# A four-layer hybrid block on one core: the engine loop written out, a new order of pieces, and a last chunk with a second V layout

## Chip, core and metric

The kernel runs on one NeuronCore of a Trainium2 chip. The metric is the device time of one execution in microseconds (us). TensorE (PE) multiplies, VectorE (DVE), ScalarE (ACT) and GpSimd (POOL) do the rest, and SyncE (SP) issues most of the transfers.

## What is computed

The input x is 8 batches x 512 tokens x 128 features, float32. Four layers follow, each added to x after a layer norm of x:

```
x = x + ssm(layernorm(x))      # 8 heads of 64 values, state 128; B and C turned by cumulative angles
x = x + ffn(layernorm(x))      # x @ ternary(W).T * alpha + bias, 128 -> 128
x = x + attn(layernorm(x))     # 16 heads of 8, over the 8 batches of each token
x = x + ffn(layernorm(x))      # the same ternary weights
```

The ssm layer is a scan over the 512 tokens of a batch (h = alpha h + beta Bx_prev + gamma Bx, y = h.C), an RMS norm and an output projection. The attention softmax has only 8 columns, the batches of one token.

## The kernel before

Every engine has a program of its own, and semaphores tie them. The tokens are cut into 4 chunks of 128 (NC = 4); a chunk has 8 tiles, one per batch, each 128 tokens x 128 features. A tile is worked in two **units** of four heads, so a chunk has 16 units (UNITS) and unit k belongs to tile k//2. The ssm of a unit on TensorE: project_b and project_c (three passes of 128x512 each), ScalarE turns the result by cosine and sine (L922, L937), GpSimd adds the two parts (L630, L631), TensorE transposes (L1679), scores (L1816); VectorE scans the decays into a mask (scan, L1282) from a band that GpSimd made (band_of, L651) and multiplies the scores by it (weigh_scores, writes mmat, L1290); TensorE makes outputs (L1829, L1835) and states (L1848); VectorE adds up y (L1301, L1304) and the state (L1321). After two units ScalarE squares y (L958), VectorE sums the squares (L1330), TensorE projects out (L1858, L1859), and VectorE copies the result to oraw (o_out, L1334).

Layers 2 to 4 of a chunk are small **pieces** (norms, transposes, FFN products, score products "prod", their sums "red", softmax) that run among the units of the next chunk. The table PLACE (L66) gives each a place in units; at 16 and over it falls in the next chunk. step() of each engine lays down the calls of one unit and, between them, at_span() lets the pieces of a stretch in. run_chunks (L130) calls step():

```python
    with eng.Fori(1, NC - 1) as c:
        for k in range(UNITS):
            step(c, k, pieces)
```

Chunk 0 and chunk 3 are written out; chunks 1 and 2 are two passes of one hardware loop, on all five engines (SP's at L516). In the loop some waits and addresses come from registers.

Chunk 3 has no chunk after it. Its first FFN and its attention start as **head pieces** (names with h, by pairs p of tiles): rms root, x1, norm hnorm0, transpose hT0, FFN hF, hadd, hnorm1, hT1, then hKV, hQ and the products hprod and sums hred of the scores that need no tile of pair 3. What is left is the **ending**, written by hand: the lists TV, TA, TP, TG number the steps of VectorE, ScalarE, TensorE and GpSimd. scores_of and sum_copied finish the scores, weights() makes the softmax in two halves, values_of(s) (DVE L1598, POOL L801) multiplies weights by V into a 128x1024 tile for each batch tile s, and add_rows (L2049) lets TensorE add its 8 parts with 8 matmuls against the identity. GpSimd makes the values of tiles 2 to 5, VectorE those of 0, 1, 6, 7; the last two VectorE first folds from 1024 to 256 (L1603), so that they take 2 matmuls each. Then for each pair: out_of (L2054), attended (DVE L1608, L1614, L1619), a root on GpSimd (L809), norm_of (L1625), turn_pair (L2073), ffn_of (L2054), add_to_x and the store.

Warm-up matmuls (keep_warm, L1679 with only ident) keep TensorE occupied while it waits.

## Time and profile before

| | us |
|---|---|
| three runs | 607.63, 604.37, 606.64; median 606.64 |
| profiled execution | 608.52 |
| its span | 606.8 |
| PE busy | 526.3 (87%) |
| ACT busy | 482.5 (80%) |
| DVE busy | 470.1 (77%) |
| POOL busy | 433.8 (71%) |
| mean granted TensorE clock | 0.966 |

The span is what the profiler saw from the first to the last event on the core; 1.7 us of the execution lie around it. In the rows below a timeline line has its start in us, its length in us, engine, line, operation, tiles, forms, and in brackets how long the engine was idle before it and what ended that; a window line has its ends and length, then busy us (instructions) of PE, PEld (weight loads), DVE, ACT, POOL, then the mean clock, the DMA share and GB/s. Busy shares are means over stretches that differ: set-up to 45 us, chunk 0 to about 140, chunks 1 and 2 of about 140 each, chunk 3 with the head pieces to about 560, then the ending.

### The profile page before, as it was taken

What the parts mean: (1) busy time and instruction counts of PE and PEld (TensorE: products, weight loads), DVE (VectorE), ACT (ScalarE), POOL (GpSimd) and SP (SyncE); (2) the same over time, 40 slices, a digit from 0 to 9 for tenths busy, and PEclk for the clock granted to TensorE, in tenths of its full rate; (3) what the DMA queues carried; (4) which work ended last, traced back from release to release, by engine and by line L of the source; (5) the groups of instructions that cost most, each with busy time, mean ns of one, the idle gap of its engine ahead of it and who ended that gap; (6) DMA issues with size and microseconds to landing.
All of it is one profiled execution on the core that took longest, in us unless ns stands there. A gap on an engine that the chain in (4) does not pass through costs nothing. (4 is left out here: it accounts for less than half of the span.)

```text
span 606.8 us, 13457 instructions
## 1 busy us (share of the span) xinstructions
PE 526.3 (87%) x3932; PEld 437.9 (72%) x3932; DVE 470.1 (77%) x1093; ACT 482.5 (80%) x1478; POOL 433.8 (71%) x568
## 2 busy tenths in 40 slices
PE   5978999999999898896999888899998786879287
PEld 4866888888887777785887777788777575766175
DVE  6666576687659999983767999997559979953995
ACT  3799999999998879695998887789999789843101
POOL 7348777878777887783678796977768876944742
PEclk9989999999999999997999999999999989987769
DMA  8841222132111112231111111232211112000001
GB/s 198 219 112 50 75 74 81 59 99 76 59 44 52 59 59 59 62 102 35 56 59 59 59 53 31 93 94 93 88 31 54 63 41 66 27 18 2 1 0 36
DMA packets 52309, 39.44 MB, mean 65 GB/s; under 512 B 7301, under 2 KB 48010, under 8 KB 52234
## 3 DMA queue, kind: packets, MB, share of 16 engines
q1 hardware_dynamic: 45898, 35.39, 19.7%
q10 hardware_dynamic: 6336, 3.15, 1.8%
q8 instruction: 36, 0.59, 0.4%
q14 instruction: 39, 0.32, 0.2%
HBM read 33.44 MB, written 4.46 MB: 62 GB/s over the span
## 5 line engine op out<-in xcount | busy, mean ns | idle before, releaser
L937 ACT ACTIVATE turned<-ps,sct 128x128 f32<-128x128 f32 x376 | 110.7, 446 | 0.0
L922 ACT ACTIVATE turned<-ps,sct 128x128 f32<-128x128 f32 x368 | 103.3, 434 | 6.4 <-DMA sct<-packed 3.9
L1282 DVE TENSOR_TENSOR_SCAN lmat<-arow,band 128x512 f32<-128x512 f32 x64 | 86.5, 1356 | 5.6 <-POOL band L651 3.6
L630 POOL TENSOR_TENSOR cn<-turned 128x256 f32<-128x256 f32 x64 | 54.4, 850 | 39.4 <-ACT turned L937 39.4
L1290 DVE TENSOR_TENSOR mmat<-ps,lmat 128x512 f32<-128x512 f32 x64 | 43.9, 685 | 46.4 <-PE ps L1816 46.4
L630 POOL TENSOR_TENSOR bn<-turned 128x256 f32<-128x256 f32 x64 | 52.9, 826 | 36.7 <-PE ps L1848 25.1
L1816 PE MATMUL ps<-cT,bT 128*128 128x128 f32 x512 | 69.4, 278 | 8.2 <-DVE state L1321 5.8
L1816 PEld LDWEIGHTS ps<-cT,bT 128*128 128x128 f32 x512 | 63.2, 191 | 16.4 <-issue 14.9
L828 ACT ACTIVATE area<-ps 128x256 f32<-128x256 f32 (+1 forms) x68 | 34.6, 565 | 42.8 <-PE ps L2049 14.0
L1721 PE MATMUL ps<-w_sel_hi,xt_hi 128*128 128x512 f32 x128 | 59.1, 462 | 1.4 <-ACT turned L937 1.4
L1848 PE MATMUL ps<-wu,bn 128*128 128x128 f32 x384 | 54.6, 286 | 4.0 <-DVE mmat L1290 3.9
L828 ACT ACTIVATE cT<-ps 128x512 f32<-128x512 f32 x64 | 43.7, 683 | 13.8 <-PE ps L1679 13.3
L1848 PEld LDWEIGHTS ps<-wu,bn 128*128 128x128 f32 x384 | 47.3, 194 | 9.5 <-issue 9.3
L631 POOL TENSOR_TENSOR bn<-turned 128x256 f32<-128x256 f32 x64 | 53.1, 830 | 0.0
L1679 PE MATMUL ps<-ident,cn 128*128 128x128 f32 x256 | 40.4, 281 | 14.4 <-ACT bT L828 14.1
L828 ACT ACTIVATE bT<-ps 128x512 f32<-128x512 f32 x64 | 43.5, 679 | 11.5 <-PE ps L1679 11.5
L651 POOL TENSOR_TENSOR band<-bandm,sct 128x512 f32<-128x512 f32 x48 | 50.3, 1049 | 1.3 <-DMA sct<-packed 1.3
L1723 PE MATMUL ps<-w_sel_hi,xt_lo 128*128 128x512 f32 x128 | 50.8, 397 | 0.0
L1722 PE MATMUL ps<-w_sel_lo,xt_hi 128*128 128x512 f32 x128 | 50.7, 396 | 0.0
L631 POOL TENSOR_TENSOR cn<-turned 128x256 f32<-128x256 f32 x64 | 49.9, 780 | 0.0
L1829 PE MATMUL ps<-mmat,u_nat 128*64 128x128 f32 x512 | 42.6, 288 | 6.9 <-DVE mmat L1290 6.6
L1679 PEld LDWEIGHTS ps<-ident,cn 128*128 128x128 f32 x256 | 28.7, 142 | 21.9 <-issue 21.3
(271 smaller groups left out, 1430.1 us busy)
## 6 DMA issues: line engine op xcount, KB each, us to landing
arow<-alpha_rows SPq DMA_DIRECT2D x32, 512.0 KB, 3.7
drow<-decay_rows SPq DMA_DIRECT2D x64, 128.0 KB, 3.1
area<-in_L_attn_a_x_dram SPq DMA_DIRECT2D x4, 512.0 KB, 6.1
xT_rows<-turned SPq DMA_DIRECT2D x4, 512.0 KB, 4.9
xt<-xT_rows SPq DMA_DIRECT2D x32, 64.0 KB, 2.5
area<-in_L_attn_a_x_dram ACTq DMA_DIRECT2D x6, 256.0 KB, 3.0
out_dram<-area ACTq DMA_DIRECT2D x6, 256.0 KB, 2.4
area<-L_attn_a_sel_proj_w_dram SPq DMA_DIRECT2D x2, 512.0 KB, 6.4
```

What stands on the lines that cost most here:

```text
L630: pool.tensor_tensor(out[:, 0], zc[:, 0], zs[:, 1], ALU.subtract)
L631: return pool.tensor_tensor(out[:, 1], zc[:, 1], zs[:, 0], ALU.add)
L828: return act.activation(dst, src, ACT.Copy)
L922: last = act.activation(dst[h][:, N * q:N * q + N], bank(BK_B)[:, N * q:N * q + N], ACT.Copy, scale=scalars(c, k)[:, at + HH * h + q:at + ...
L937: last = act.activation(dst[h][:, N * q:N * q + N], bank(BK_C)[:, N * q:N * q + N], ACT.Copy, scale=scalars(c, k)[:, at + HH * h + q:at + ...
L1282: dve.tensor_tensor_scan(lmat[h], arow[i2][:, HH * P * h:HH * P * (h + 1)], band[h], 0.0, ALU.mult, ALU.add).then_inc(l_dve, 1)
L1679: last = pe.transpose(bank(k)[:, into + P * q:into + P * q + P], s, ident[:])
L1721: pe.matmul(out, xt_hi[i2], hi, start=True, stop=False)
L1722: pe.matmul(out, xt_hi[i2], lo, start=False, stop=False)
L1723: pe.matmul(out, xt_lo[i2], hi, start=False, stop=True).then_inc(signal, 1)
L1816: last = pe.matmul(bank(BK_G)[:, P * q:P * q + P], bT[h][:, P * q:P * q + P], cT[h][:, P * q:P * q + P], start=True, stop=True)
L1848: last = pe.matmul(bank(BK_G)[:, at:at + P], bn[h][:, N * q:N * q + N], wu[h][:, 2 * PD * (q // 2):2 * PD * (q // 2) + 2 * PD], start=True ...
```

## The change

1. The loop over chunks 1 and 2 is written out on all five engines. No register is computed and no branch taken there; every wait is for a constant. The load of ScalarE's function table, which stood in the first step of the loop body and ran in each pass, now stands once, ahead of the first softmax exponential, in chunk 1.
2. The table PLACE and the order of calls in step() are new. VectorE's o_out stands before weigh_scores in even units, its scan of an even unit at the end of the odd one before, GpSimd's band_of one place earlier, TensorE's outputs always before states. Many head pieces of chunk 3 are earlier.
3. In the last chunk ScalarE writes V out a second time as vals_er, with the 8 batches innermost. It does so in f_hvals, after a wait until the stores of chunk 2 have landed, since vals_er lies over their rows. The values of tiles 4 to 7 are made in this layout, and VectorE sums each over the batches with one reduce (128x1024 to 128x128); TensorE then turns each with one transpose. The folds on VectorE go. GpSimd folds tiles 2 and 3 once, so that they take 4 matmuls each instead of 8.
4. Warm-up transposes: 8 before the last project_out, 24 before the ending's first rows, 4 before its second.
5. out_of and ffn_of use other PSUM banks by pair, and the ending's steps are in a new order on VectorE and TensorE.

```diff
-WARM_STATS, WARM_NORM, WARM_SCALARS, WARM_ANGLE, WARM_LAST = 4, 1, 4, 2, 1
+WARM_STATS, WARM_NORM, WARM_SCALARS, WARM_ANGLE, WARM_LAST, WARM_VALUES = 4, 1, 4, 2, 1, 2
...
-PLACE = {"hrms:0": 10.75, "hx1:0": 10.786, "rr:0": 11.296, "hroot0:0": 11.407, "hnorm0:0": 11.441,
+PLACE = {"hx1:0": 6.844, "hrms:0": 6.917, "hroot0:0": 7.444, "hnorm0:0": 9.276, "rr:0": 11.148, "hrms:1": 11.259,
...
-    with eng.Fori(1, NC - 1) as c:
+    for c in range(1, NC - 1):
...
+ON_GPSIMD_LAST = [2, 3, 4, 5]
-               ("v", 6), ("v", 7), ("a", 6), ("a", 7), ("h", 6), ("h", 7),
-               ("ao", 0), ("st", 0), ("mv", 0), ("ao", 1), ("st", 1), ("mv", 1),
-               ("xn", 0), ("xn", 1), ("ao", 2), ("st", 2), ("mv", 2), ("ao", 3), ("st", 3), ("mv", 3),
-               ("af", 0), ("af", 1), ("xn", 2), ("xn", 3), ("af", 2), ("af", 3)])
...
+        vals_er = area[:, 3072:4096].rearrange("p (e r) -> p e r", r=NB)
...
-        o_bank = [bank(BK_C), bank(BK_Y), bank(BK_C), bank(BK_Y)]
-        ffn_bank = [bank(BK_F0), bank(BK_M), bank(BK_F1), bank(BK_T)]
+        o_bank = [bank(BK_C), bank(BK_Y), bank(BK_F0), bank(BK_M)]
+        ffn_bank = [bank(BK_C), bank(BK_Y), bank(BK_F1), bank(BK_T)]
...
                 if first_chunk(c):
                     pool.wait_ge(pv, PV["packed"])
-                elif k < 0:
+                else:
                     scalars_ready(pool, c, k)
...
             def values_of(s):
                 pool.wait_ge(tv, TV["wp", s // 4])
...
+                else:
+                    tick(pool.tensor_tensor(wide[s].rearrange("p (h d r) -> p h d r", r=NB, d=AD),
+                                            w_last[:, s - 2, :].rearrange("p (h r) -> p h r", r=NB).unsqueeze(2).broadcast_to([P, AH, AD, NB]),
+                                            vals_er.rearrange("p (h d) r -> p h d r", d=AD), ALU.mult), ("v", s))
...
+            def fold(s):
+                pool.wait_ge(tg, TG["v", s])
+                tick(pool.tensor_tensor(wide[s][:, 0:512], wide[s][:, 0:512], wide[s][:, 512:1024], ALU.add), ("a", s))
...
             values_of(2)
+            fold(2)
             values_of(3)
+            fold(3)
             values_of(4)
             values_of(5)
...
             def f_hvals(c, p):
                 act.wait_ge(hp[p], HEAD_P["KV"])
-                evac(vals_last[:, pair(p), :], kv_bank[p].rearrange("p (s e) -> p s e", s=2)[:, :, D:2 * D]).then_inc(ha[p], 1)
+                rows = kv_bank[p].rearrange("p (s e) -> p s e", s=2)[:, :, D:2 * D]
+                evac(vals_last[:, pair(p), :], rows)
+                for g in range(2):
+                    act.wait_ge(rows_free[g], 16 * NC)
+                evac(vals_er[:, :, pair(p)].rearrange("p e s -> p s e"), rows).then_inc(ha[p], 1)
...
@@ VectorE, step(), even units, both forms cut to the calls @@
-                    scan(c, k)
-                    y_of(c, k - 2)
-                    weigh_scores(c, k - 1)
-                    o_out(c, (k - 4) // 2)
+                    y_of(c, k - 2)
+                    o_out(c, (k - 4) // 2)
+                    weigh_scores(c, k - 1)
@@ TensorE, step(), odd units, likewise @@
-                    states(c, k - 1)
-                    outputs(c, k - 1)
+                    outputs(c, k - 1)
+                    states(c, k - 1)
...
-            def fold(s, n, before, name):
-                dve.wait_ge(tv, TV[before, s])
-                end_tick(dve.tensor_tensor(wide[s][:, 0:n], wide[s][:, 0:n], wide[s][:, n:2 * n], ALU.add), (name, s))
...
+            def sum_values(s):
+                if s in (4, 5):
+                    dve.wait_ge(tg, TG["v", s])
+                else:
+                    dve.wait_ge(tv, TV["v", s])
+                end_tick(dve.tensor_reduce(xn[:, s], wide[s].rearrange("p (e r) -> p e r", r=NB), AX.X, ALU.add), ("r", s))
 
...
-            fold(6, 512, "v", "a")
-            fold(7, 512, "v", "a")
-            fold(6, 256, "a", "h")
-            fold(7, 256, "a", "h")
+            sum_values(4)
+            sum_values(5)
+            sum_values(6)
             attended(0)
+            sum_values(7)
             attended(1)
             norm_of(0)
+            attended(2)
             norm_of(1)
-            attended(2)
             attended(3)
             add_to_x(0, ffn_bank[0], "F", "af")
+            norm_of(2)
             add_to_x(1, ffn_bank[1], "F", "af")
-            norm_of(2)
             norm_of(3)
             add_to_x(2, ffn_bank[2], "F", "af")
...
+                if in_ending(c) and b == NB - 1:
+                    for signal, count in ((y_dve, UNITS * NC), (ysq_act, NT)):
+                        pe.wait_ge(signal, count)
+                        keep_warm(WARM_LAST, BK_T)
...
-                if s in (2, 3, 4, 5):
-                    pe.wait_ge(tg, TG["v", s])
+                if s in ON_GPSIMD_LAST:
+                    pe.wait_ge(tg, TG["v" if n == NB else "a", s])
                 else:
-                    pe.wait_ge(tv, TV["v" if n == NB else "h", s])
+                    pe.wait_ge(tv, TV["v", s])
...
+            def turn_row(p, s):
+                pe.wait_ge(tv, TV["r", s])
+                at = P * (s % 2)
+                return pe.transpose(acc_bank[p][:, at:at + P], xn[:, s], ident[:])
+
...
+            for name in ("sum", "rec", "w"):
+                pe.wait_ge(tv, TV[name, 0])
+                keep_warm(WARM_VALUES, BK_C)
             add_rows(0, 0, NB)
+            pe.wait_ge(tv, TV["sub", 1])
+            keep_warm(WARM_LAST, BK_C)
             end_tick(add_rows(0, 1, NB), ("acc", 0))
-            add_rows(1, 2, NB)
-            end_tick(add_rows(1, 3, NB), ("acc", 1))
+            bias_of(o_bank[0], BIAS_O)
+            bias_of(o_bank[1], BIAS_O)
+            add_rows(1, 2, NB // 2)
+            end_tick(add_rows(1, 3, NB // 2), ("acc", 1))
             out_of(0)
             out_of(1)
-            pe.wait_ge(tv, TV["v", 1])
-            bias_of(ffn_bank[0], BIAS_F)
-            bias_of(ffn_bank[1], BIAS_F)
-            add_rows(2, 4, NB)
-            end_tick(add_rows(2, 5, NB), ("acc", 2))
-            pe.wait_ge(tv, TV["w", 1])
-            bias_of(ffn_bank[2], BIAS_F)
-            add_rows(3, 6, 2)
-            end_tick(add_rows(3, 7, 2), ("acc", 3))
-            bias_of(ffn_bank[3], BIAS_F)
-            out_of(2)
-            out_of(3)
-            turn_pair(0)
-            turn_pair(1)
-            ffn_of(0)
-            ffn_of(1)
-            turn_pair(2)
-            turn_pair(3)
-            ffn_of(2)
-            ffn_of(3)
+            for p in (2, 3):
+                bias_of(o_bank[p], BIAS_O)
+            for p in (2, 3):
+                turn_row(p, 2 * p)
+                end_tick(turn_row(p, 2 * p + 1), ("acc", p))
+                out_of(p)
+            for p in (0, 1):
+                pe.wait_ge(tv, TV["ao", p])
+                bias_of(ffn_bank[p], BIAS_F)
+            for p in (2, 3):
+                bias_of(ffn_bank[p], BIAS_F)
+            for p in range(4):
+                turn_pair(p)
+                ffn_of(p)
```

How the instructions stand. First TensorE where chunk 1 begins, before:

```order
L1679 MATMUL ps<-ident,bn 128x128 x4
L136 UNCONDITIONAL_BRANCH
L136 ISA
L1679 MATMUL ps<-ident,area 128x128 x4
L1824 REGISTER_ALU
L1825 REGISTER_ALU
L243 REGISTER_ALU
L1829 MATMUL ps<-mmat,u_nat 64x128 x4
L243 REGISTER_ALU
L1835 MATMUL ps<-cT,state 64x128 x4
L1848 MATMUL ps<-wu,bn 128x128 x4
L1804 REGISTER_ALU
```

and after:

```order
L1744 MATMUL ps<-w_sel_lo,xt_hi 128x512
L1745 MATMUL ps<-w_sel_hi,xt_lo 128x512
L1701 MATMUL ps<-ident,area 128x128 x4
L1701 MATMUL ps<-ident,bn 128x128 x4
L1851 MATMUL ps<-mmat,u_nat 64x128 x4
L1857 MATMUL ps<-cT,state 64x128 x4
L1870 MATMUL ps<-wu,bn 128x128 x4
L1701 MATMUL ps<-ident,cn 128x128 x4
```

The branch, the ISA row (of the loop) and the register rows are gone; outputs (L1829, L1835, now L1851, L1857) and states (L1848, now L1870) keep their order in this unit, and the transposes of area (L1679, now L1701) have moved before those of bn.

Second, VectorE after the last unit of chunk 3; L1452 (now L1466) is hadd, L1446 (now L1460) is hnorm0 and hnorm1, L1461 (now L1475) is a product of scores. Before, from hadd of pair 2 on:

```order
L1452 TENSOR_TENSOR small<-ps,small 128x256
L1431 BN_STATS stats_h<-small 128x6 x2
L1434 MEMSET carrier 128x1
L1436 BN_AGGR mv_h<-stats_h 128x2 x2
L1446 TENSOR_SCALAR area<-small,mv_h,rs_h 128x128 x2
L1452 TENSOR_TENSOR small<-ps,small 128x256
L1431 BN_STATS stats_h<-small 128x6 x2
L1434 MEMSET carrier 128x1
L1436 BN_AGGR mv_h<-stats_h 128x2 x2
L1446 TENSOR_SCALAR area<-small,mv_h,rs_h 128x128 x2
L1461 TENSOR_TENSOR area<-ps,area 128x1024
L1461 TENSOR_TENSOR area<-ps,area 128x512
```

and after, from the end of x1 of pair 3 on:

```order
L1448 MEMSET carrier 128x1
L1450 BN_AGGR mv_h<-stats_h 128x2 x2
L1460 TENSOR_SCALAR area<-small,mv_h,rs_h 128x128 x2
L1466 TENSOR_TENSOR small<-ps,small 128x256
L1445 BN_STATS stats_h<-small 128x6 x2
L1448 MEMSET carrier 128x1
L1450 BN_AGGR mv_h<-stats_h 128x2 x2
L1475 TENSOR_TENSOR area<-ps,area 128x512
L1475 TENSOR_TENSOR area<-ps,area 128x1024
L1480 TENSOR_REDUCE area<-area 128x2x4x16
L1480 TENSOR_REDUCE area<-area 128x2x2x16
L1460 TENSOR_SCALAR area<-small,mv_h,rs_h 128x128 x2
```

hadd of pair 2 now stands before the copy of the last oraw and so no longer between x1 of pair 3 and hnorm0 of pair 3; the products hprod4 and hprod3 and two sums have moved before hnorm1 of pair 3.

Third, VectorE in the ending, from the values of tiles 6 and 7 on. Before:

```order
L1598 TENSOR_TENSOR arow<-ps,area 128x1024 x2
L1603 TENSOR_TENSOR arow<-arow 128x512 x2
L1603 TENSOR_TENSOR arow<-arow 128x256 x2
L1608 TENSOR_TENSOR small<-ps,small 128x256
L1614 BN_STATS stats_f<-small 128x6 x2
L1617 MEMSET carrier 128x1
L1619 BN_AGGR mv_f<-stats_f 128x2 x2
L1608 TENSOR_TENSOR small<-ps,small 128x256
L1614 BN_STATS stats_f<-small 128x6 x2
L1617 MEMSET carrier 128x1
L1619 BN_AGGR mv_f<-stats_f 128x2 x2
L1625 TENSOR_SCALAR area<-small,mv_f,rs_f 128x128 x4
```

and after:

```order
L1616 TENSOR_TENSOR arow<-ps,area 128x1024 x2
L1625 TENSOR_REDUCE area<-area 128x128 x2
L1625 TENSOR_REDUCE area<-arow 128x128
L1630 TENSOR_TENSOR small<-ps,small 128x256
L1636 BN_STATS stats_f<-small 128x6 x2
L1639 MEMSET carrier 128x1
L1641 BN_AGGR mv_f<-stats_f 128x2 x2
L1625 TENSOR_REDUCE area<-arow 128x128
L1630 TENSOR_TENSOR small<-ps,small 128x256
L1636 BN_STATS stats_f<-small 128x6 x2
L1639 MEMSET carrier 128x1
L1641 BN_AGGR mv_f<-stats_f 128x2 x2
```

Four folds (L1603) have given way to four reduces (L1625), and the last of these stands after the first attended.

## Rows read from the trace of the kernel before

**Rows 1.** Windows: each engine's busy us (instructions), clock, DMA; chunks 1, 2, ending
```profile
149.20:281.20 132.00, 117.16 (x919) 97.68 (x920) 110.89 (x242) 112.16 (x348) 99.07 (x125) 0.99 0.19 60
289.50:421.50 132.00, 122.20 (x965) 102.38 (x964) 114.23 (x259) 115.13 (x358) 103.34 (x130) 1.00 0.22 66
560.00:607.00 47.00, 28.53 (x177) 23.90 (x176) 35.77 (x69) 6.75 (x18) 23.07 (x17) 0.82 0.04 12
```

**Rows 2.** Timeline of VectorE: mmat of units around chunk boundaries (start, us, idle before)
```profile
140.34 0.69 DVE L1290 TENSOR_TENSOR mmat<-ps,lmat 128x512 f32<-128x512 f32 x1 [0.17 <-PE ps L1816]
...
149.22 0.69 DVE L1290 TENSOR_TENSOR mmat<-ps,lmat 128x512 f32<-128x512 f32 x1 [0.28 <-PE ps L1816]
...
276.30 0.68 DVE L1290 TENSOR_TENSOR mmat<-ps,lmat 128x512 f32<-128x512 f32 x1
...
289.49 0.69 DVE L1290 TENSOR_TENSOR mmat<-ps,lmat 128x512 f32<-128x512 f32 x1 [0.26 <-PE ps L1816]
...
414.32 0.68 DVE L1290 TENSOR_TENSOR mmat<-ps,lmat 128x512 f32<-128x512 f32 x1
...
421.49 0.69 DVE L1290 TENSOR_TENSOR mmat<-ps,lmat 128x512 f32<-128x512 f32 x1 [0.27 <-PE ps L1816]
```

**Rows 3.** Timeline of TensorE, ScalarE and GpSimd where chunk 1 becomes chunk 2
```profile
276.58 0.33 PE L1679 MATMUL ps<-ident,area 128*128 128x128 f32 x1 [2.09 <-issue]
...
279.83 0.80 PE L1679 MATMUL ps<-ident,area 128*128 128x128 f32 x3 [2.92 <-issue]
...
277.24 1.28 ACT L828 ACT_TABLE_LOAD   x1 [1.50 <-issue]
...
284.71 0.73 POOL L630 TENSOR_TENSOR bn<-turned 128x256 f32<-128x256 f32 x1 [10.19 <-PE ps L1848]
```

**Rows 4.** Timeline of ScalarE, first step of chunk 1
```profile
143.48 1.28 ACT L828 ACT_TABLE_LOAD   x1
```

**Rows 5.** The page's costliest groups: outputs and band (count, busy, mean ns, idle before)
```profile
L1829 PE MATMUL ps<-mmat,u_nat 128*64 128x128 f32 x512 | 42.6, 288 | 6.9 <-DVE mmat L1290 6.6
...
L651 POOL TENSOR_TENSOR band<-bandm,sct 128x512 f32<-128x512 f32 x48 | 50.3, 1049 | 1.3 <-DMA sct<-packed 1.3
```

**Rows 6.** Timeline of TensorE and VectorE, last tile of chunk 3
```profile
536.21 1.06 PE L1858 MATMUL ps<-w_out,yT 128*128 128x128 f32 x8
...
543.31 2.08 PE L1858 MATMUL ps<-w_out,yT 128*128 128x128 f32 x8 [2.69 <-DVE ysum L1330]
...
547.23 0.61 DVE L1424 SCALAR_TENSOR_TENSOR small<-oraw,rr_h,small 128x128 f32<-128x128 f32 x2 [1.08 <-POOL rr_h L722]
...
552.32 0.42 DVE L1452 TENSOR_TENSOR small<-ps,small 128x256 f32<-128x256 f32 x1 [2.56 <-PE ps L1938]
...
553.46 0.57 DVE L1446 TENSOR_SCALAR area<-small,mv_h,rs_h 128x128 f32<-128x128 f32 x2
```

**Rows 7.** Timeline of VectorE and ScalarE, from pair 3 to the first late scores
```profile
558.33 0.60 DVE L1446 TENSOR_SCALAR area<-small,mv_h,rs_h 128x128 f32<-128x128 f32 x2 [1.08 <-POOL rs_h L730]
...
561.86 1.82 DVE L1461 TENSOR_TENSOR area<-ps,area 128x1024 f32<-128x1024 f32 x2 [2.93 <-PE ps L1956]
...
564.88 0.38 ACT L828 ACTIVATE q_last<-ps 128x256 f32<-128x256 f32 x1 [0.41 <-PE ps L1956]
...
568.98 1.22 DVE L1461 TENSOR_TENSOR area<-ps,area 128x1024 f32<-128x1024 f32 x1 [0.19 <-issue]
```

**Rows 8.** Timeline of VectorE and GpSimd, last values to the end
```profile
570.23 1.22 DVE L1466 TENSOR_REDUCE area<-area 128x128 f32<-128x1024 f32 x1
...
584.43 3.90 POOL L801 TENSOR_TENSOR area<-w_last,area 128x1024 f32<-128x1024 f32 x2 [4.34 <-DVE w_last L1578]
...
586.98 3.16 DVE L1603 TENSOR_TENSOR arow<-arow 128x512 f32<-128x512 f32 x4
...
598.20 0.42 DVE L1608 TENSOR_TENSOR small<-ps,small 128x256 f32<-128x256 f32 x1 [3.08 <-PE ps L2054]
...
603.55 0.94 DVE L1608 TENSOR_TENSOR small<-ps,small 128x256 f32<-128x256 f32 x2 [1.20 <-PE ps L2054]
```

187 lines of the change are left out of this document (94 added, 93 removed), and 65 rows, old and new, of tables (PLACE, TV).

## Prediction

> **What bounds the kernel now.** I read four views in this order: busy time by windows, to see what is full in each chunk; VectorE's timeline around each chunk boundary; the timelines of all engines across the last tile of chunk 3; and those of the ending. In the windows [rows 1] no engine is full in chunks 1 and 2: of 132.0 us, TensorE is busy 117 and 122, ScalarE 112 and 115, VectorE 111 and 114. Two chunks with 5 us difference in TensorE work take the same 132.0 us, so TensorE's sum alone doesn't set the pace; it is the round of waits from unit to unit, and a queue change pays or costs where the reader would look for it last. In the ending [rows 1] TensorE is busy 28.5 of 47 us at a clock of 0.82, VectorE 35.8: there VectorE leads, with some waits.
>
> The unit rows [rows 2] show what the windows hide. The multiply of scores (mmat) starts in the last unit of a chunk and in the first of the next at 276.30 and 289.49 (13.19 us apart) between chunks 1 and 2, at 414.32 and 421.49 (7.17) between 2 and 3, where the same pieces run but no branch is taken, and at 140.34 and 149.22 (8.88) where the loop is entered. First unit to first unit is 140.27 and 132.00 us; the difference is 8.27. So each pass back costs 8.3 us. The engines say what it is [rows 3]: TensorE sits idle 2.09 and 2.92 us "issue", that is for nothing the profile shows, inside a group of four transposes; ScalarE has 1.50 us of the same and a table load of 1.28; GpSimd waits 10.19 us for TensorE. The page "Runtime: NRT & Kernel Launch" of the Trainium skill (Instruction fetch mechanics) says that a taken branch out of the fetched window has to fetch its target before it can go on, and that straight code is prefetched at a mostly hidden cost; the stall at the branch agrees, and boundary 2 to 3 shows none in straight code.
>
> **The change, part by part.** All against the profiled execution, 608.52 us.
>
> 1. Loop written out: the back edge goes, **-8.3**. At the entry, 8.88 - 7.17 = 1.7 us are there to gain; of it the table load of 1.28 [rows 4] is on ScalarE, which has no idle time there. It moves to where VectorE is ahead of it in chunk 1, and one of its two runs goes. I take **-1.3** (bounds: 0 and -1.7). Register instructions go in 32 units; the page gives them no time: nothing taken.
>
> 2. New order and table. Unit order stays nearly the same. On VectorE o_out goes ahead of mmat in even units, on TensorE outputs ahead of states in all. o_out waits for project_out, which TensorE issues ahead of the scores that mmat waits for, so this costs the copy alone, hidden where mmat waits anyway. GpSimd's band (1.05 us [rows 5]) is made earlier, and costs only if it delays an add. Moved pieces keep their durations. Each of three chunks may move by some us either way: VectorE idles 132.0 - 114.2 = 17.8 us in chunk 2 [rows 1]. That is an upper bound for a gain in a chunk, and nothing in the rows gives a direction; nearest is that chunks 1 and 2, with different piece loads, took the same time. I take **0**, with 3 us to either side per chunk for three chunks.
>
> 3. Last tile. The last project_out takes 2.08 us, the one before 1.06 [rows 6]: it came after a wait of 2.69 and ran at half clock. Warmed, it gives **-1.0**. Then x1 of pair 3 (547.23) is ready for its norm about 1.3 + 1.1 us later, 549.6, but the norm starts at 553.46, since VectorE first waits 2.56 us for hadd of pair 2 [rows 6]. That wait goes. What is late next is TensorE: behind project_out stand hT1 of pair 1, hQ of pair 0, hKV and hQ of pair 1 and 12 warm-ups. Before, 7.8 us lay between the end of the norm (554.0) and the product that ended VectorE's wait at 561.86 [rows 7]: about 2.0 for transpose, copy and product of pair 3, and five hKV or hQ groups, so 1.16 each. So three groups (3.5), a transpose with its copy (0.8) and 12 warm-ups (1.6, at 1.06 for eight [rows 6]) are 5.9 us from 544.7, and pair 3's transpose can start at about 550.6 against 554.0. hadd of pair 3 comes at 552.5; only hT1, hKV and hQ of pair 2 (0.8 and two groups, 3.1) stand before hprod4 and hprod3, so these start at about 555.6 against 561.86 [rows 7]. Here the change gives something back: hnorm1 of pair 3 now stands behind two products (1.82 [rows 7]) and two sums (as long again), and comes at 559.2 against 558.33, 0.9 us later. But before, TensorE was then busy with pairs 1 and 2 until 561.9; now it is free, and pair 3's K and Q come 3 us earlier. The norm (0.6) and three sums (3.5 us) follow on VectorE, and the first late scores come at 563.3 against 568.98 [rows 7]: **-5.7 in all, the -1.0 within it**. q_last (564.88) comes at about 562.9, so GpSimd's two scores stay ahead of their readers. Bounds: -3 if TensorE runs this at half clock, -8 if the warm-ups cost nothing. ScalarE's four second copies of V (0.4 to 0.7 us each) and the wait for chunk 2's stores lie in ScalarE's idle time; uncovered they cost 2 us.
>
> 4. Ending. Until v7 VectorE does the same work in the same order, with one wait less between parts: 0. Behind it (586.98 [rows 8]) it did four folds (3.16), then waited 3.08 for pair 2's product and 1.20 for the last [rows 8]. Now: four reduces of 128x1024 at 1.22 [rows 8], less overlap 4.8; four attended at 1.14 (552.32 to 553.46 is such a triple [rows 6]), 4.6; four norms at 0.60 [rows 7], 2.4; four final adds at 0.47 [rows 8], 1.8. That is 13.6 with no wait, so 600.6, and the last norm is still followed by transpose, copy and product, 1.2 as before: 601.8 against 603.55 + 0.94 = 604.5, **-2.7**. It is covered if GpSimd has v4 and v5 by 590: before 584.43 + 3.90 = 588.3 [rows 8], and its two new folds (128x512, like the band's 1.05 [rows 5]) end before the weights of half 1. Bounds: 0, and -4.3 if both waits go with nothing in return. The sum uses the row. A rule of the Trainium skill speaks against the reduce: "VectorE: DVE Perf Modes" (Rules for kernel authors) calls tensor_reduce the slowest VectorE operation and advises to restructure. The row differs: 1.22 us for 1024 elements [rows 8], the same as the multiply at 568.98 [rows 7]. Were the reduce twice as slow, the sum would lose 4.9 and the ending would end 2 us later than before.
>
> Sum: -8.3 - 1.3 - 5.7 - 2.7 = -18.0, so 590.5 for an execution like the profiled one. That one lies 1.9 above the median of the three runs (606.64), so I forecast **588.6**.
>
> **Rivals.**
> - *The new order also gains* (chance 0.16): less waiting for scores, 2 to 3 us per chunk: 580 to 583. For: 17.8 us idle on VectorE. Against: TensorE waited only 6.6 us for mmat in all 64 units [rows 5].
> - *Last tile and ending give back* (0.20): TensorE stays at half clock through pair 3, reduces or the new V layout are slow, or ScalarE's wait for the stores delays the last square. Then only the loop's 9.6 and a rest remain: 592 to 598. For: clock 0.82 in the ending. Against: the reduce's row.
> - *The straight code stalls by itself* (0.05): the fetch of more code costs as much as the branch: 597 to 600. Against: no such stall at 414 to 421.
> - *The order costs* (0.06): 2 to 4 us per chunk, 594 to 600.
> - *Slower* (0.04): TensorE's outputs now stand ahead of states everywhere, and so wait for mmat, with the next unit's transposes behind them. Now 9 waits, 6.6 us in all [rows 5], 0.73 each. Should each of 48 units wait 0.73 us, that is +28: 616. It decides from a loss of 18.0 + 3, 0.44 us per unit, or 29 waits more. Against: in half of the units outputs stand there already.
>
> The forecast itself, 584 to 592, has 0.49.
>
> **Chances and range.** About 0.5% (3 us) is what a measurement of this kernel tells from no change. Faster: 0.49 + 0.16 + 0.20 + 0.05 and nearly all of "costs", 0.94; same 0.02; slower 0.04. The range, 580 to 598, leaves out a better order than 3 us per chunk (0.03) and the last of the rivals (some 0.12).
>
> **What would show it.** First units of chunks 132 us apart with no "issue" wait and no table load at the start of chunk 1 (step 1); the same distances off by 1 to 3 us (step 2); project_out of the last tile at 1.1 us, hnorm0 of pair 3 within 3 us of x1, the first late scores 18 us behind the last oraw, which is now at 547.2 - 1.1 - 0.3 = 545.8 [rows 6], 23.1 us ahead of them (step 3); no wait over 1.5 us on VectorE between v7 and the end, and 14.8 us from v7's end to VectorE's last add against 17.5 (step 4). The prediction is wrong if the first units stay 140 us apart, or if units of chunk 3 take longer than before.

## The result, and the profile after

The changed kernel takes **599.88 us** (median of 7 runs, 598.03 to 601.9); before takes 606.64 (7 runs, 602.45 to 608.08). The ratio is 0.9906, with a 95% interval from 0.988 to 0.9932: 6.8 us faster, where 18.0 were forecast. The measured time lies outside the range of 580 to 598.

The profiled execution of the changed kernel has 598.75 us and a span of 597.0. Before, span and execution were 606.8 and 608.52. So the two profiled executions differ by 9.8 us, 3 more than the medians, since one lies 1.9 us above its median and the other 1.1 below. VectorE's first mmat starts between 50.05 and 52.45 us in the 18 profiled executions of this document, with no relation to what the kernels change, so a difference of 1 to 2 us between two single executions says nothing of the edit. Stage by stage, from the start of one VectorE instruction to the next (unit numbers count from 0 to 63; "end" is the end of VectorE's last add):

| from, to | before | after | forecast of the difference | measured |
|---|---|---|---|---|
| mmat of unit 0, unit 15 | 89.37 | 89.36 | 0 | 0 |
| 15, 16 (loop entry) | 8.88 | 7.62 | -1.3 | -1.3 |
| 16, 32 (chunk 1 and the back edge) | 140.27 | 131.95 | -8.3 | -8.3 |
| 32, 48 (chunk 2) | 132.00 | 132.03 | 0 | 0 |
| 48, 63 (chunk 3) | 116.93 | 121.39 | 0 | **+4.5** |
| 63, first reciprocal | 36.44 | 30.38 | -5.7 | -6.1 |
| first reciprocal, second | 8.32 | 8.92 | 0 | **+0.6** |
| second reciprocal, end | 21.31 | 22.69 | -2.7 | **+1.4** |

The first mmat also starts 0.5 us earlier. The forecast's four terms came out at -8.3, -1.3, -6.1 and, for the ending, +2.0; the part that was put at nothing cost 4.5. The sixth row goes past the point at which step 3 of the forecast ends: from mmat of unit 63 to the first late scores 30.56 us became 24.08, -6.5, and 0.4 us were lost again before the reciprocal.

The windows of chunk 2 and of the end, columns as in [rows 1]:

```profile
279.40:411.40 132.00, 122.32 (x965) 102.42 (x964) 113.86 (x259) 114.75 (x357) 101.22 (x129) 1.00 0.22 66
...
575.80:597.00 21.20, 12.63 (x51) 8.37 (x49) 12.53 (x41) 2.69 (x7) 5.63 (x9) 0.61 0.09 26
```

Chunk 2 is as full as before [rows 1]. The last 21 us run at a clock of 0.61.

VectorE's timeline, the same units as in [rows 2] and then units 61 to 63:

```profile
139.78 0.68 DVE L1304 TENSOR_TENSOR mmat<-ps,lmat 128x512 f32<-128x512 f32 x1
...
147.40 0.69 DVE L1304 TENSOR_TENSOR mmat<-ps,lmat 128x512 f32<-128x512 f32 x1 [0.27 <-PE ps L1838]
...
272.25 0.68 DVE L1304 TENSOR_TENSOR mmat<-ps,lmat 128x512 f32<-128x512 f32 x1
...
279.35 0.69 DVE L1304 TENSOR_TENSOR mmat<-ps,lmat 128x512 f32<-128x512 f32 x1 [0.26 <-PE ps L1838]
...
404.29 0.68 DVE L1304 TENSOR_TENSOR mmat<-ps,lmat 128x512 f32<-128x512 f32 x1
...
411.38 0.69 DVE L1304 TENSOR_TENSOR mmat<-ps,lmat 128x512 f32<-128x512 f32 x1 [0.27 <-PE ps L1838]
...
517.57 0.68 DVE L1304 TENSOR_TENSOR mmat<-ps,lmat 128x512 f32<-128x512 f32 x1
...
525.80 0.69 DVE L1304 TENSOR_TENSOR mmat<-ps,lmat 128x512 f32<-128x512 f32 x1 [2.30 <-PE ps L1838]
...
532.77 0.69 DVE L1304 TENSOR_TENSOR mmat<-ps,lmat 128x512 f32<-128x512 f32 x1 [0.33 <-PE ps L1838]
```

The three boundaries are now 7.62, 7.10 and 7.09 us long. Unit 62 comes 8.23 us after unit 61, with VectorE idle 2.30 for scores. Before, the mmat of unit 61 started at 526.24 and that of unit 62 came 5.2 us after it:

```profile
531.43 0.69 DVE L1290 TENSOR_TENSOR mmat<-ps,lmat 128x512 f32<-128x512 f32 x1 [1.02 <-PE ps L1816]
```

So 3.0 of the 4.5 us of chunk 3 lie in this one interval. In the changed kernel, the timelines of ScalarE and TensorE show what TensorE waited for there:

```profile
517.63 0.88 ACT L1049 ACTIVATE small<-small,sh_h,rs_h 128x128 f32<-128x128 f32 x2 [2.69 <-POOL sh_h L734]
...
521.32 0.66 ACT L841 ACTIVATE bT<-ps 128x512 f32<-128x512 f32 x1
...
522.12 0.63 PE L1701 MATMUL ps<-ident,cn 128*128 128x128 f32 x4 [1.42 <-ACT bT L841]
```

ScalarE stood 2.69 us before a head norm, for GpSimd's shift. Behind it in its queue were the turn of B of unit 63 and the copy bT of unit 62, and TensorE's transposes of C waited for that copy.

GpSimd was late for a reason of its own. Two of its instructions on 128x2 took 1.02 and 1.15 us, where the same two took 0.20 and 0.19 for the pair before (at 512.73 and 512.89). They ran while VectorE did two scans, and each ended where a scan ended:

```profile
514.37 2.31 DVE L1296 TENSOR_TENSOR_SCAN lmat<-arow,band 128x512 f32<-128x512 f32 x2
...
514.54 1.02 POOL L727 TENSOR_TENSOR rs_h<-mv_h,eps_ln 128x2 f32<-128x2 f32 x1 [0.51 <-DVE mv_h L1450]
515.52 1.15 POOL L729 TENSOR_SCALAR sh_h<-mv_h 128x2 f32<-128x2 f32 x1
```

That is 1.8 of ScalarE's 2.69 us. The same pair of long instructions (1.02 and 1.14 to 1.15 us) stands there in all nine profiles that keep this root and these scans in their new places. No experiment moved a scan; e9_norm0b below moved the root away from them and met another wait. So what the kernel would take without this meeting alone is not shown.

The other 1.5 us are spread out: 0.8 in units 48 to 53 and 0.7 in units 53 to 61. In the latter VectorE is nearly full, busy 61.6 of 64.3 us after and 60.2 of 63.6 before, so head pieces that are moved there have little idle time to run in.

The last tile, to lay beside [rows 6] and [rows 7]:

```profile
537.69 1.16 PE L1884 MATMUL ps<-w_out,yT 128*128 128x128 f32 x8
...
540.48 0.61 DVE L1438 SCALAR_TENSOR_TENSOR small<-oraw,rr_h,small 128x128 f32<-128x128 f32 x2 [1.08 <-POOL rr_h L723]
...
542.98 0.61 DVE L1460 TENSOR_SCALAR area<-small,mv_h,rs_h 128x128 f32<-128x128 f32 x2 [1.08 <-POOL rs_h L731]
...
548.77 1.82 DVE L1475 TENSOR_TENSOR area<-ps,area 128x512 f32<-128x512 f32 x2 [1.60 <-PE ps L1982]
...
552.36 0.60 DVE L1460 TENSOR_SCALAR area<-small,mv_h,rs_h 128x128 f32<-128x128 f32 x2
...
553.01 0.68 PE L1956 MATMUL ps<-ident,area 128*128 128x128 f32 x2 [3.94 <-DVE area L1460]
...
556.85 1.23 DVE L1475 TENSOR_TENSOR area<-ps,area 128x1024 f32<-128x1024 f32 x1 [0.51 <-ACT area L841]
```

project_out is at full clock (1.16 us). The norm of pair 3 (542.98) starts 2.50 us after its x1 (540.48), where it was 6.2 [rows 6]. The products start at 548.77, the second norm stands behind them at 552.36, TensorE waits 3.94 us for it, and the first late scores start at 556.85.

The ending, beside [rows 8]:

```profile
573.16 4.67 POOL L807 TENSOR_TENSOR area<-w_last,area 128x1024 f32<-128x1024 f32 x2 [1.72 <-DVE w_last L1592]
...
575.73 1.21 DVE L1625 TENSOR_REDUCE area<-area 128x128 f32<-128x1024 f32 x1
...
577.87 1.22 DVE L1625 TENSOR_REDUCE area<-area 128x128 f32<-128x1024 f32 x1 [0.93 <-POOL area L807]
...
585.57 0.69 PE L2100 MATMUL ps<-ident,area 128*128 128x128 f32 x2
...
586.73 1.22 PE L2084 MATMUL ps<-w_of,area 128*128 128x128 f32 x4 [0.47 <-ACT area L841]
...
587.98 0.42 DVE L1630 TENSOR_TENSOR small<-ps,small 128x256 f32<-128x256 f32 x1 [1.14 <-PE ps L2084]
...
590.10 0.42 DVE L1630 TENSOR_TENSOR small<-ps,small 128x256 f32<-128x256 f32 x1 [1.18 <-PE ps L2084]
...
594.34 0.42 DVE L1630 TENSOR_TENSOR small<-ps,small 128x256 f32<-128x256 f32 x1 [1.70 <-PE ps L2084]
```

GpSimd's two values in the new layout take 4.67 us against 3.90 [rows 8], and VectorE waits 0.93 for the second. One value takes 2.35 to 2.37 us in the new layout and 1.97 in the old one, in before, the changed kernel, e3, e10 and e15 alike, so this is the layout's price. At the end TensorE's two transposes take 0.69 and four products 1.22, both at half clock, with 0.47 idle between them for ScalarE's copy. The final adds start 2.12 us apart (587.98, 590.10, 592.22, 594.34), each after a wait of over a microsecond.

### The profile page after: what moved, and what is told of

Its sections match the earlier page's. It is cut to its first block, busy times and chain, and to the rows that moved or that the text cites. A ratio compares the mean times of both kernels' runs of the same rounds, so it can differ in the third digit from the quotient of the medians.

```text
span 597.0 us, 12795 instructions
## 1 busy us (share of the span) xinstructions
PE 524.3 (88%) x3916; PEld 432.6 (72%) x3916; DVE 473.0 (79%) x1093; ACT 481.9 (81%) x1481; POOL 436.1 (73%) x570
## 4 chain that ended last, share of the span: by engine, by line
PE 42%; DVE 34%; ACT 9%; issue 9%; POOL 5%; DMA 1%; DVEq 1%; SPq 0%; ACTq 0%; POOLq 0%
PE ps L1701 7%; PE ps L1870 5%; PE ps L1838 5%; DVE lmat L1296 5%; PE ps L1851 3%; DVE area L1403 3%; PE ps L1743 3%; PE ps L1745 3%; PE ps L1744 3%; DVE state L1335 3%; PE ps L1884 2%; DVE mmat L1304 2%; DVE area L1386 2%; ACT turned L950 2%; ACT turned L935 2%
## 5 line engine op out<-in xcount | busy, mean ns | idle before, releaser
L1296 DVE TENSOR_TENSOR_SCAN lmat<-arow,band 128x512 f32<-128x512 f32 x64 | 82.4, 1291 | 3.6 <-POOL band L652 3.6
L631 POOL TENSOR_TENSOR bn<-turned 128x256 f32<-128x256 f32 x64 | 49.7, 776 | 38.2 <-PE ps L1870 31.7
L1304 DVE TENSOR_TENSOR mmat<-ps,lmat 128x512 f32<-128x512 f32 x64 | 43.9, 686 | 41.4 <-PE ps L1838 41.3
L631 POOL TENSOR_TENSOR cn<-turned 128x256 f32<-128x256 f32 x64 | 50.3, 786 | 29.9 <-ACT turned L950 29.6
L841 ACT ACTIVATE area<-ps 128x256 f32<-128x256 f32 (+1 forms) x72 | 37.9, 576 | 39.0 <-PE ps L2100 8.1
L632 POOL TENSOR_TENSOR bn<-turned 128x256 f32<-128x256 f32 x64 | 58.0, 906 | 0.0
L1851 PE MATMUL ps<-mmat,u_nat 128*64 128x128 f32 x512 | 42.1, 285 | 15.5 <-DVE mmat L1304 15.5
L1870 PE MATMUL ps<-wu,bn 128*128 128x128 f32 x384 | 55.6, 288 | 0.0
L1870 PEld LDWEIGHTS ps<-wu,bn 128*128 128x128 f32 x384 | 46.5, 191 | 8.2 <-issue 8.2
L632 POOL TENSOR_TENSOR cn<-turned 128x256 f32<-128x256 f32 x64 | 51.9, 811 | 0.0
L1701 PE MATMUL ps<-ident,cn 128*128 128x128 f32 x256 | 39.4, 276 | 9.9 <-ACT bT L841 8.7
L1851 PEld LDWEIGHTS ps<-mmat,u_nat 128*64 128x64 f32 x512 | 26.6, 136 | 27.3 <-DVE mmat L1304 20.7
```

Source lines behind the costliest of these rows:

```text
L631: pool.tensor_tensor(out[:, 0], zc[:, 0], zs[:, 1], ALU.subtract)
L632: return pool.tensor_tensor(out[:, 1], zc[:, 1], zs[:, 0], ALU.add)
L841: return act.activation(dst, src, ACT.Copy)
L1296: dve.tensor_tensor_scan(lmat[h], arow[i2][:, HH * P * h:HH * P * (h + 1)], band[h], 0.0, ALU.mult, ALU.add).then_inc(l_dve, 1)
L1701: last = pe.transpose(bank(k)[:, into + P * q:into + P * q + P], s, ident[:])
L1851: last = pe.matmul(bank(BK_Y)[rows, at:at + P], u_nat[i2][:, PD * (HH * h + q):PD * (HH * h + q + 1)], mmat[h][:, P * q:P * q + P], start= ...
```

## The experiments

Stages were measured in all kernels as in the table above. "Order" is the new table PLACE with the new step() of all engines, "ending" all parts of the change from the second V layout on.

### The change taken apart: loop alone, loop and order, loop and ending, all

e1_loop is before with this edit, and the same on SP's engine:

```diff
-    with eng.Fori(1, NC - 1) as c:
+    for c in range(1, NC - 1):
```

> Before with nothing but its loop over chunks 1 and 2 written out. My theory (the branch back costs 8.3 us and the table load at the loop's head 1.3, whatever else changes): 9.6 us faster than before, 0.984, first units of chunks 132 us apart, 7.1 us from the last unit of a chunk to the first of the next. Rival (the stall is not the branch's, the written-out code stalls elsewhere or the gain is given back in chunk 3): 0 to 4 us faster.

> Before with the loop written out and the new order (table PLACE, step() of all engines), without the new ending and without the warm-ups. My theory (the head pieces that moved into chunk 3 slow its last units by 4 to 5 us, and the last tile's stretch, from the last mmat to the first late scores, gains 6): within 1 us of the kernel with the loop alone; units 48 to 63 take 121 us against 117. Rival (the order costs in chunks 1 and 2 too, or nowhere): 3 us slower than the loop alone, or 6 faster.

> Before with the loop written out and the new ending with its warm-ups, banks and second V layout, in the old order of pieces. My theory (the new ending as such gives nothing or loses 1 us, because TensorE runs at half clock behind the reduces, one pair after another; the warmed project_out gives 1): 0 to 1 us faster than the loop alone. Rival (the ending gives the 2.7 us that I forecast): 3 to 4 us faster.

> The changed kernel again, beside the others on one chip: 1 to 1.6% faster than before, 590 to 601 us. By my theory it is within 1 us of the kernel with loop and order; by the rival, in which the ending gives something, it is 3 us faster than that.

| | median us | ratio to before, interval | 48 to 63 | 63 to first reciprocal | to second | to end |
|---|---|---|---|---|---|---|
| loop alone | 597.78 | 0.9853, 0.9813 to 0.9893 | 115.66 | 35.13 | 8.32 | 21.53 |
| loop and order | 599.19 | 0.9891, 0.9851 to 0.993 | 121.06 | 31.43 | 8.33 | 21.04 |
| loop and ending | 597.08 | 0.9846, 0.981 to 0.9882 | 114.61 | 33.70 | 8.92 | 22.71 |
| all (changed kernel) | 600.10 | 0.9904, 0.9869 to 0.994 | 120.30 | 30.39 | 8.92 | 22.70 |

The loop alone gives the whole gain: 8.1 us between the medians. Against it the other three differ by +1.4, -0.7 and +2.3 us, and none of these is clear of the scatter: the runs of the loop alone go from 595.1 to 600.0, those of the changed kernel from 598.2 to 601.5, and in the two profiled executions the changed kernel is the faster one (598.24 against 599.96). So neither order nor ending adds a gain, and that they cost something is not shown by these four. Stage by stage the new order loses 5.4 us in units 48 to 63 and gains 3.7 in the last tile and 1.1 at the loop's entry.

VectorE's mmat in the kernel with the loop alone:

```profile
141.59 0.69 DVE L1290 TENSOR_TENSOR mmat<-ps,lmat 128x512 f32<-128x512 f32 x1
...
150.32 0.69 DVE L1290 TENSOR_TENSOR mmat<-ps,lmat 128x512 f32<-128x512 f32 x1 [0.27 <-PE ps L1816]
...
275.31 0.68 DVE L1290 TENSOR_TENSOR mmat<-ps,lmat 128x512 f32<-128x512 f32 x1
...
282.49 0.69 DVE L1290 TENSOR_TENSOR mmat<-ps,lmat 128x512 f32<-128x512 f32 x1 [0.27 <-PE ps L1816]
```

The back edge is gone (7.18 us). But the entry is still 8.73 us long, though no table load is there: behind the set-up ScalarE loads once, at 200.18, in chunk 1. So the load at the entry cost 0.15 us (8.88 less 8.73). What shortens the entry to 7.62 us in both kernels with the new order is the order. The back edge gives 6.0 us between units 31 and 32 and 2.1 more between units 16 and 31 (127.08 against 124.99), which I had not looked at. These belong to the back edge too: they lie in one interval, but for 0.2 us, from unit 30 to unit 31, which took 10.78 us and takes 8.53 now. Before, VectorE made unit 31's mmat in the first step of the next pass, and had stood idle for nothing the profile shows ahead of a scan there:

```profile
274.08 1.53 DVE L1282 TENSOR_TENSOR_SCAN lmat<-arow,band 128x512 f32<-128x512 f32 x1 [1.99 <-issue]
```

### Chunk 3: three tries at one wait

e5_norm0 moves the second norm of pair 0 behind ScalarE's turn of B (the four entries picked out of PLACE):

```diff
-"hnorm1:0": 13.621, "hout1:0": 13.655, "hT1:0": 13.795, "hKV:0": 14.211
+"hnorm1:0": 14.2, "hout1:0": 14.23, "hT1:0": 14.17, "hKV:0": 14.39
```

> The changed kernel with the second norm of pair 0 and what hangs on it (hnorm1:0, hout1:0, hT1:0, hKV:0) half a unit later, behind ScalarE's turn of B for unit 62 and 63 and not ahead of it. My theory (in chunk 3 ScalarE stands 2.7 us before this norm for GpSimd's root, and the turn of B, the transposes and the scores of the last units wait behind it): units 58 to 63 go back from 41 to about 38 us, 2 to 3 us faster than the changed kernel. Rival (the head pieces cost by their sheer number, wherever they stand): no gain, and the head's later K only shifts the loss.

It ran at 601.57 us (0.9929, 0.99 to 0.9958), no faster than the changed kernel, where 2 to 3 us were expected, and units 58 to 63 take 41.59 us. GpSimd, ScalarE and TensorE:

```profile
517.01 0.73 POOL L631 TENSOR_TENSOR bn<-turned 128x256 f32<-128x256 f32 x1
...
514.15 2.21 ACT L935 ACTIVATE turned<-ps,sct 128x128 f32<-128x128 f32 x8
...
523.13 0.44 PE L1956 MATMUL ps<-ident,small 128*128 128x128 f32 x2 [2.39 <-ACT small L1049]
```

The turn of B now starts at 514.15, 2.9 us before unit 61's mmat, where it came 1.75 behind it. GpSimd's add of unit 62 still stood behind two roots until 517.01 (with the same two long instructions beside VectorE's scans, 1.02 and 1.15 us), and TensorE waited 2.39 us for the norm I had moved, with the scores behind it. One wait was exchanged for another.

e9_norm0b moves that chain later on all engines (root 14.3, norm 14.4, transpose 14.4, hKV 14.65).

> The changed kernel with the chain of pair 0's second norm later on every engine: GpSimd's root behind the adds of unit 62, ScalarE's norm behind its turns, TensorE's transpose behind the scores of unit 62. In the run before only ScalarE's part was moved and the wait went over to TensorE (2.39 us before the transpose, with the scores behind it). My theory (this one chain, put ahead of work of units 61 and 62, is what chunk 3 lost): units 58 to 63 take 38 to 39 us against 41.6, 2.5 us faster than the changed kernel. Rival (the sum of the moved head pieces is the cost): 41 us or more, no gain.

598.68 us (0.9874, 0.9845 to 0.9904), which is not clear of the changed kernel's 600.10; units 58 to 63 take 41.69 where 38 to 39 were expected. Unit 62 came 4.63 us after unit 61, as wanted; unit 63 came 10.16 after that. VectorE:

```profile
523.19 0.66 DVE L1304 TENSOR_TENSOR mmat<-ps,lmat 128x512 f32<-128x512 f32 x1
...
531.34 0.69 DVE L1375 TENSOR_TENSOR area<-ps,area 128x512 f32<-128x512 f32 x1 [5.77 <-PE ps L1920]
```

It stood 5.77 us for the last FFN of chunk 2, which TensorE made after hKV of pair 0 and two head transposes, with unit 63's transposes behind them.

e12_oldhead puts all head pieces back at their old places and keeps the rest.

> The changed kernel with the head pieces at their old places in the table, all else of the new order kept. My theory (moved head pieces cost chunk 3 what they give the last tile): units 48 to 63 take 116 to 117 us against 121, from oraw to the first reciprocal 26.5 us against 24.0, 2 us faster than the changed kernel in all. Rival (the new order of calls in step() costs in chunk 3): 119 to 121 us.

602.90 us (0.9955, 0.9933 to 0.9976), slower than the changed kernel, where I expected 2 us less. My theory fell: units 48 to 63 take 122.02 us, as with the new places (116 to 117 expected), while the stretch from oraw is back at 26.55 us. So the head places give the last tile 2.5 us and alone do not cost chunk 3 its 5. Here ScalarE waited 2.64 us for TensorE's head transpose before hout0 of pair 0, again with the turn of B of unit 63 behind it:

```profile
518.61 0.38 ACT L841 ACTIVATE small<-ps 128x256 f32<-128x256 f32 x1 [2.64 <-PE ps L1956]
```

e13_turn and e14_turn_old test what both have in common: ScalarE's new place for the turns of B, which the list of the change does not name. The new step() has the first behind all pieces of an odd unit and the second in the next unit. In chunk 3 both go ahead of the odd unit's last pieces, in e13 with the new head places and in e14 with the old ones. That is earlier than in the kernel before, where they stood between these pieces, with the copy bT of the next unit behind them; the old place itself was not tried. These lines are cut out of the edit:

```diff
                     if ok(k + 1, 1):
                         c_turn(c, k + 1, 1)
+                    if last and ok(k + 2, 1):
+                        b_turn(c, k + 2, 0)
+                        b_turn(c, k + 2, 1)
                     at_span(pieces, c, k, 0.552, 0.862, first)
```

> The changed kernel with one part of ScalarE's old order back in chunk 3: the turns of B of the unit two ahead stand together ahead of the pieces at the end of an odd unit, not the first behind them and the second in the next unit. My theory (in the last units these turns wait behind head pieces that themselves wait; they release GpSimd's adds and so the next scores): units 58 to 63 take 39 us or less against 41.6, 2 us faster than the changed kernel. Rival (GpSimd's roots or TensorE's hKV ahead of the transposes hold the same units, as in the two runs that moved pair 0's norm): 41 us or more.

> The same order of ScalarE's turns in chunk 3 and the head pieces at their old places. My theory (with both back, nothing of what moved stands ahead of the last units' turns): units 58 to 63 take 38 to 39 us, and the last tile's stretch from oraw stays 26.5 us, 2.5 us faster than the kernel with the old head places alone. Rival (another engine's new order costs): 41 us.

| | median us | ratio, interval | 48 to 53 | 53 to 58 | 58 to 63 |
|---|---|---|---|---|---|
| before | 606.64 | | 41.12 | 37.81 | 38.00 |
| loop alone | 597.78 | 0.9853, 0.9813 to 0.9893 | 41.11 | 36.54 | 38.01 |
| changed, profile of the first table | | | 41.89 | 38.89 | 40.61 |
| changed, beside the loop alone | 600.10 | 0.9904, 0.9869 to 0.994 | 41.84 | 36.91 | 41.55 |
| e12 old head places | 602.90 | 0.9955, 0.9933 to 0.9976 | 41.90 | 38.82 | 41.30 |
| e13 turns ahead | 602.22 | 0.9927, 0.9902 to 0.9952 | 45.43 | 39.48 | 40.64 |
| e14 both | 605.75 | 0.9981, 0.9954 to 1.0009 | 45.43 | 38.99 | 38.59 |

Only with both back are the last five units at 38.6 us, as I expected for e14; e13 alone leaves 40.6, where I expected 39 or less, and e12 alone 41.3. So either cause by itself, turns of B that come late or head pieces put ahead of what the next unit needs, is enough to hold the last units. The early turns cost 3.5 us in units 48 to 53 (45.43 against 41.9, in both), so both kernels are slower, e13 than the changed kernel and e14 than e12, where 2 and 2.5 us less were expected. What waits in units 48 to 53 was not followed.

Units 53 to 58 took 36.9 and 38.9 us in two executions of one kernel, and 38.8 to 39.5 in these three, so a difference of 2 us there can't be laid to an edit. Most of it is one interval, unit 55 to 56, with 7.90 us in the first profile of the changed kernel and 6.13 in the second, and TensorE's clock in it:

```profile
468.90:476.80 7.90, 6.42 (x35) 5.39 (x36) 6.18 (x10) 5.35 (x16) 7.90 (x7) 0.64 0.14 38
...
469.30:475.50 6.20, 4.70 (x38) 3.88 (x38) 6.17 (x10) 5.10 (x14) 6.20 (x5) 1.00 0.03 8
```

The second execution had its stretch at half clock some microseconds earlier (0.78 from 461.5 to 469.3), where no unit was kept waiting by it.

### The last tile: is it the clock

e8_loop_warm is the kernel with the loop alone plus the 8 warm-ups ahead of the last project_out.

> Before with the loop written out and the 8 warm-ups ahead of the last project_out, nothing else. My theory (in the kernel with the new ending the stretch from the last oraw to the first reciprocal took 26.5 us against 28.8 because the warm-ups keep TensorE at full clock through hF, hKV): 26.5 us here too, 2 us faster than the loop alone. Rival (it was another part of the new ending, or chance of the clock): 28.8 us, no change.

595.21 us (0.9832, 0.9788 to 0.9875), 2.6 less than the loop alone, and from the last oraw to the first reciprocal 26.55 us against 28.82, as the theory said. Counted from unit 63 the gain is only 1.4 us (33.68 against 35.13): with the loop alone the last project_out happened to run at full clock without any warm-up (1.16 us), and with them it took 1.78. The same four products and four hKV products, with the loop alone and then with the warm-ups:

```profile
538.18 1.22 PE L1938 MATMUL ps<-w_of,small 128*128 128x128 f32 x4
...
539.87 2.08 PE L1947 MATMUL ps<-w_qkv,small 128*128 128x256 f32 x4
```

```profile
535.16 0.71 PE L1942 MATMUL ps<-w_of,small 128*128 128x128 f32 x4
...
536.12 1.13 PE L1951 MATMUL ps<-w_qkv,small 128*128 128x256 f32 x4
```

1.22 and 2.08 us became 0.71 and 1.13.

In the new order the warm-ups do something else. This is the last project_out of the kernel with loop and order and no warm-ups:

```profile
537.75 1.96 PE L1858 MATMUL ps<-w_out,yT 128*128 128x128 f32 x8 [1.99 <-DVE ysum L1330]
```

It ran at half clock, but the products behind it were at full clock all the same (0.71 us at 541.36), and from oraw to the first reciprocal that kernel took 24.11 us, the changed one with warm-ups 24.05. There the warm-ups give 1.0 us ahead of oraw (63 to oraw 7.32 and 6.33) and nothing behind it.

The kernel with loop and warm-ups took 19.43 us from the second reciprocal to the end, where the loop alone, with the same instructions there, took 21.53 and before 21.31. Nothing was changed in that part. The clock there was 0.92 before, 0.91 with the loop alone and 1.00 here; what decides which of them an execution gets was not tested.

### The ending: clock, pairs, folds

e7_warm_end adds 40 warm-up transposes (not 32, as its expectation counts) at TensorE's waits for the reduces and copies:

```diff
+            pe.wait_ge(tv, TV["w", 1])
+            keep_warm(2, BK_F1)
             for p in (2, 3):
                 turn_row(p, 2 * p)
+                keep_warm(2, BK_F1)
                 end_tick(turn_row(p, 2 * p + 1), ("acc", p))
+                keep_warm(1, BK_F1)
                 out_of(p)
+                keep_warm(1, BK_F1)
```

> The changed kernel with 32 more warm-up transposes at TensorE's waits for the reduces of tiles 4 to 7. My theory (the ending lost because the matmuls that the reduces replaced had kept TensorE's clock up; it falls to half at 577 to 597 us): transposes and products of the last phase at 0.38 and 0.71 us again, 22.7 becomes about 21 us from the second reciprocal to the end, 1.5 us faster. Rival (VectorE's reduces set the end, the clock is no matter): no change, or 0.5 us slower by warm-ups in the way.

595.81 us (0.9831, 0.9787 to 0.9875), 4 us faster than the changed kernel; from the second reciprocal to the end 19.16 us against 22.69. The window behind the values, and TensorE in it:

```profile
576.80:595.00 18.20, 12.59 (x91) 9.77 (x90) 12.47 (x41) 2.68 (x7) 5.74 (x9) 0.94 0.10 30
```

```profile
587.45 0.38 PE L2100 MATMUL ps<-ident,area 128*128 128x128 f32 x2
...
588.30 0.71 PE L2084 MATMUL ps<-w_of,area 128*128 128x128 f32 x4 [0.47 <-ACT area L841]
```

The clock is 0.94 where it was 0.61, transposes and products take 0.38 and 0.71 us, and a pair takes 1.41 us (589.05, 590.46, 591.86 for the final adds) instead of 2.12. The gain is 3.5 us in this stretch, more than twice what I expected, since products and transposes of the attended rows were slow as well.

e6_pairs only turns the order of the last steps:

```diff
-            for p in range(4):
-                turn_pair(p)
-                ffn_of(p)
+            for p in (0, 2):
+                turn_pair(p)
+                turn_pair(p + 1)
+                ffn_of(p)
+                ffn_of(p + 1)
```

> The changed kernel with the last transposes and products by two pairs again (turn 0, turn 1, FFN 0, FFN 1, then 2 and 3). My theory (TensorE stands 0.47 us in every pair for ScalarE's copy and does the rest at half clock, 2.12 us per pair, four pairs in a row): from the second reciprocal to the end 21.6 us against 22.7, 1.1 us faster. Rival (the end is set by VectorE's adds and norms, not by TensorE's chain): no change.

596.93 us (0.9856, 0.9809 to 0.9903); 20.61 us from the second reciprocal to the end, 2.1 less where I expected 1.1. Still at half clock, but with ScalarE's copies covered by the second pair's transposes:

```profile
584.57 1.11 PE L2100 MATMUL ps<-ident,area 128*128 128x128 f32 x4
...
585.74 2.07 PE L2084 MATMUL ps<-w_of,area 128*128 128x128 f32 x8
```

e10_nofold takes GpSimd's two folds out, so that TensorE adds 8 parts of tiles 2 and 3.

> The changed kernel without GpSimd's two folds of tiles 2 and 3, so that TensorE adds 8 parts of each. My theory (VectorE's subtraction of the maximum, both operands in SBUF, ran 1.28 us instead of 0.69 because GpSimd worked beside it, where before GpSimd had just ended): from the first to the second reciprocal 8.3 us against 8.9, and GpSimd's values of tiles 4 and 5 no earlier; 0.6 us faster. Rival (it is the second V layout or the layout of the weights, or the extra matmuls take the gain back): no change.

598.56 us (0.9871, 0.9835 to 0.9906). VectorE's subtraction for the second half, in the changed kernel and then without the folds:

```profile
569.02 1.28 DVE L1588 TENSOR_TENSOR area<-area,amax 128x512 f32<-128x512 f32 x1
```

```profile
570.67 0.69 DVE L1586 TENSOR_TENSOR area<-area,amax 128x512 f32<-128x512 f32 x1
```

1.28 us became 0.69, and the stretch between the reciprocals is 8.33 us again. In the changed kernel GpSimd's product for tile 3 runs until 569.75, since the first fold has pushed it back, and the second fold starts at 569.84; so the subtraction stood beside mostly that product and then the fold. Without the folds GpSimd's product had ended at 570.06, before the subtraction. An earlier subtraction of the same size shows the same without any fold: 1.11 us beside a GpSimd product in both kernels (560.08 and 561.74), 0.69 before (572.21), when GpSimd had just ended. The folds slowed VectorE by 0.6 us and relieved a TensorE that was waiting anyway. Between the medians 1.5 us are measured, within their scatter, of which only this 0.6 and 0.7 less at the end can be seen in the stages.

### Put together

e11_best has the loop written out, the old order and the new ending with pairs and warm-ups; e15_best is that without the folds; e16_after_cured is the changed kernel with all three.

> Before with the loop written out and the new ending, in the old order of pieces, with the last transposes and products by two pairs and the warm-ups at the waits for the reduces. The parts as measured in the other kernels give: units 48 to 63 115 us, to oraw 7.2, to the first reciprocal 26.5, to the second 8.9, to the end 18.5; 3 us faster than the kernel with the loop and the two warm-ups where that one had no luck with its clock: 593 us, 0.979 of before. Rival (two cures of the same wait don't add up): 595 us.

> The loop written out, the old order, the new ending with products by two pairs and warm-ups at its waits, and now without GpSimd's folds. My theory (the fold's cost is VectorE's slowed subtraction): 8.3 us instead of 8.9 from the first to the second reciprocal, 0.6 us faster than with the folds, 593 us, 0.978 of before. Rival: TensorE's 8 more matmuls stand ahead of the reduces' transposes and take it back, no change.

> The changed kernel as it is with all three cures of its ending (two pairs, warm-ups, no folds). My theory: the sum of the parts, units 48 to 63 121 us, 6.3 to oraw, 24.0 to the first reciprocal, 8.3, and 18.5 to the end: 595 us, 1 to 2 us slower than the same cures on the old order, because the new order loses 6 us in units 48 to 63 and gains 2.5 behind them, 1.1 at the loop's entry and 1.7 in chunks 1 and 2. Rival (the new order pays where the ending is cured): 593 us or less.

| | median us | ratio, interval | 48 to 63 | 63 to first reciprocal | to second | to end |
|---|---|---|---|---|---|---|
| e11_best | 593.50 | 0.9796, 0.9766 to 0.9826 | 114.89 | 33.64 | 8.92 | 18.67 |
| e15_best | 592.66 | 0.9783, 0.9751 to 0.9816 | 114.55 | 33.73 | 8.33 | 19.56 |
| e16_after_cured | 596.34 | 0.9833, 0.9797 to 0.9868 | 120.42 | 30.22 | 8.33 | 19.56 |

Both kernels on the old order beat before and the changed kernel; e15_best is 2.2% faster than before (1.8 to 2.5%). Without the folds the stretch between the reciprocals is 0.6 us shorter, as expected, and the end 0.9 us longer, so that cure is worth nothing on its own here (0.8 us between medians, within what these can tell). The changed kernel with the same cures stays 3.7 us behind by the medians, with hardly an overlap of the runs (593.7 to 598.6 against 592.0 to 595.1): the new order costs on balance. The stages of the two profiled executions account for 1.0 us of it (5.9 lost in units 48 to 63, 3.5 gained behind them, 1.1 at the entry, 0.2 in chunk 1). Another 2.2 us of their difference lie ahead of the first mmat, where the kernels do not differ, so how much the order costs is known less well than that it does.

And what the new ending is worth at a full clock can be read against e8_loop_warm, which has the old one: from the first reciprocal to the end that kernel took 27.75 us in its profile, e11_best 27.59 and e15_best 27.89, all three with a clock of 1.00 from the second reciprocal on. The new ending's own gain is about nothing. Its kernels have the lower medians (593.50 and 592.66 against 595.21), and their granted clock over the whole span is the higher one in most executions (0.979 to 0.991 against 0.974 to 0.986); that they keep it more often because of their warm-ups is likely but not shown.

## Why the prediction was wrong

**Step 1, the loop: right, one reason wrong.** -8.3 was measured as -8.3 in the profile of the changed kernel and -8.1 with the loop alone. That straight code would not stall by itself holds: chunks 1 and 2 take 131.95 and 132.03 us. The Trainium skill's "Runtime: NRT & Kernel Launch" (Instruction fetch mechanics) calls the cost of streaming a long kernel mostly hidden, and these times agree. (In the old order they go up to 133.1 in single executions; the interval from unit 43 to 44 with the loop alone, 9.61 us for 8.71, had a clock of 0.85 for 1.00.) The -1.3 at the entry came out in size but not for its reason. I put the table load's 1.28 us on the path because ScalarE had no idle time before it; without it the entry is 0.15 us shorter. A full engine need not be the one that the next unit waits for. The new order gave the other 1.1 us.

**Step 2, the order: wrong, and this is the first large error.** "I take 0, with 3 us to either side per chunk" holds for chunks 1 and 2 and fails in chunk 3, which lost 4.5 us against before and 4.6 to 5.7 against the loop alone, where 3 was the bound. I had counted head pieces only where they left the last tile, not where they went: step 3 took 5.7 us out of the tail without asking what stands behind these pieces at their new place. There ScalarE waits for GpSimd, GpSimd for VectorE's statistics and beside VectorE's scans (1.8 us), and TensorE for ScalarE, each with the next unit's work behind. "Moved pieces keep their durations" failed there too, for two of GpSimd's. e12 to e14 show that ScalarE's turns of B, which the forecast did not look at, have a share in it. The rival "the order costs" named the sign but spread the cost evenly over three chunks.

**Step 3, the last tile: right.** -6.1 against -5.7 by the table, -6.5 at the forecast's own end, the first late scores, which come 17.7 us behind the last oraw where 18 were given. project_out, the norm and the products came as worked out. The second norm came behind the products, 11.9 us after x1 by the rows after, as forecast in kind; TensorE had by then no work, waited 3.94 us and ran at half clock. The -1.0 for the warmed project_out is what the warm-ups give in the new order (31.43 against 30.39 us from unit 63). But the 2.08 us that it was read from belong to an execution and not to the kernel: with the loop alone the same project_out ran at full clock with no warm-up.

**Step 4, the ending: wrong, the second large error.** Forecast -2.7, measured +2.0. VectorE's part was right: four reduces at 1.21 to 1.22 us, so the row held, and the rule against tensor_reduce of the Trainium skill ("VectorE: DVE Perf Modes", Rules for kernel authors) did not decide here. Three things were left out. One: "the last norm is still followed by transpose, copy and product, 1.2 as before" took durations at full clock, from an ending in which 52 accumulating matmuls kept TensorE going. The change leaves 24 of them and four transposes, and the clock in the last 21 us is 0.61; in the window from 587 to 606.8 us of before it was 1.00. Warm-ups alone bring 3.5 us back. Two: with one pair at a time, ScalarE's copy lies bare in each; turning the order alone brings 2.1. Three: GpSimd's work beside VectorE's subtraction costs 0.6, the folds take 1.28 and 1.60 us where 1.05 was taken, and the two values in the new layout take 0.8 us more, so that VectorE waits 0.93 for the second. With warm-ups and pairs the stretch takes 18.67 us, 2.6 less than before, which looks like the forecast's 2.7; but the old ending took 19.43 where its clock was 1.00, so most of that is clock and not the reduces. My rival "last tile and ending give back" had the right mechanism (half clock) but was given 0.20, and with the loop's gain and chunk 3 untouched: 592 to 598 us. The measured time needed this rival and the order's cost together, and I had priced no such sum.

**The range.** My two mechanisms that went wrong stood as separate rivals. Together, at 4.5 and 4.7 us more than forecast, they make 597.8 on the median's basis. The rest to 599.9 is that both profiled executions lie off their medians (3.0 us), less 0.9 by which the start and the last tile came out better.

## What to carry over

Removing a loop's back edge can be priced by the same boundary elsewhere in the same program, and here that price held within 0.2 us. A piece moved out of the tail has to be costed at its new place, engine by engine, with what stands behind it there; and taking matmuls off an idling TensorE can cost its clock, so the durations in the last steps have to be priced at the clock that the new, emptier schedule will have.

## Not expected of the hardware

VectorE's subtraction of 128x512 with both operands in SBUF took 0.69 us where GpSimd had nothing to do and 1.28 beside GpSimd's product and fold, by the two rows of the experiment without folds. The other way round, GpSimd's instructions on 128x2 took 1.02 and 1.15 us beside VectorE's scans, each to the end of a scan, and 0.20 and 0.19 for the pair before. And the same instructions at the end took 21.3, 21.5 and 19.4 us in three kernels that differ only far ahead of them, with TensorE's clock at 0.92, 0.91 and 1.00.
